# A four-layer graph network on one core: positions counted earlier, index lists by DMA, own scores placed in the node stage, and a larger descriptor room

## What is computed

```python
def L0(feat, r_feat, src, dst, W1, b1, W2s, b2s, W2d, b2d, attn):   # 2 heads of 32
    en = (feat @ W2s + b2s).reshape(n, H, F)[src]
    ev = (feat @ W2d + b2d).reshape(n, H, F)[dst]
    e = jnp.sum(leaky_relu(en + ev, 0.2) * attn, axis=-1, keepdims=True)
    m = segment_max(e, dst)
    ee = jnp.exp(e - m[dst])
    alpha = ee / jnp.maximum(segment_sum(ee, dst)[dst], 1e-09)
    msg = softmax(en * r_feat * alpha, axis=-1)
    return (feat + jnp.sum(segment_sum(msg, dst), axis=1)) @ W1 + b1
def L1(x, edge_index):
    return segment_sum(x[src], dst)
def L2(h, edge_index, edge_sh, edge_radial, ...):
    # three small products give 256 weights an edge; tensor-product messages of h[src]
    return h_self + segment_sum(messages, dst) / 4
def L3(h, edge_index, w, fc_w, fc_b, bias):                          # 4 heads
    e = leaky_relu(a_src[:, src] + a_dst[:, dst] + fc_b, 0.2)
    att = softmax of e over the edges of one src
    return mean over heads of segment_sum(att * hp[:, dst, :], src) + bias
```

## Time and profile before

| | us |
|---|---|
| median of 3 runs | 11253.84 |
| the three runs | 11251.82, 11254.23, 11253.84 |
| the profiled execution, its own time | 11248.29 |
| its span in the profile | 11246.5 |
| busy: POOL, DVE | 8106.8, 6482.3 |
| busy: PE, ACT | 3535.6, 3252.6 |

### The profile page before, as it was taken

How to read it: one execution, slowest core, us unless ns; L and a number is a source line. 1 busy time by engine, 2 the same in 40 slices (tenths; PEclk the granted TensorE clock), 3 DMA queues, 4 the chain that set the end, 5 groups by cost and what they waited for, 6 DMA issues and landing times. The chain is left out here.

```text
span 11246.5 us, 94626 instructions
## 1 busy us (share of the span) xinstructions
PE 3535.6 (31%) x22146; PEld 2356.7 (21%) x22342; DVE 6482.3 (58%) x10678; ACT 3252.6 (29%) x5001; POOL 8106.8 (72%) x8498
## 2 busy tenths in 40 slices
PE   3201100056667664000000008888888200000002
PEld 2201100046666563000000003333333100000002
DVE  8738865588888885200000018999999234444442
ACT  0012221145555553011111102222222024334331
POOL 5777777647777777777777767777777577777775
PEclk6555555578888887555555558888888555555555
DMA  7124433311221111111111111111111122222222
GB/s 261 52 86 134 132 107 104 97 53 57 66 66 64 58 66 36 31 26 26 26 26 26 26 35 27 29 29 29 29 29 27 24 53 67 69 72 71 72 72 60
DMA packets 462695, 680.58 MB, mean 61 GB/s; under 512 B 263781, under 2 KB 359878, under 8 KB 424630
## 3 DMA queue, kind: packets, MB, share of 16 engines
q0 software_dynamic: 270016, 149.13, 8.4%
q10 hardware_dynamic: 67072, 346.84, 8.1%
q1 hardware_dynamic: 125558, 184.07, 4.9%
HBM read 368.75 MB, written 310.60 MB: 60 GB/s over the span
## 5 line engine op out<-in xcount | busy, mean ns | idle before, releaser
L1420 POOL DMA_INDIRECT hs<-tab_h,idx x3136 | 2978.6, 950 | 1034.0 <-issue 996.8
L1166 POOL DMA_INDIRECT by_src<-ends,pos_i x1568 | 1564.7, 998 | 643.3 <-issue 487.6
L1985 POOL DMA_INDIRECT hs<-tab_h,idx x1568 | 1480.3, 944 | 518.7 <-issue 518.7
L962 POOL DMA_INDIRECT en<-tab_s,idx x1568 | 1489.2, 950 | 500.2 <-issue 462.8
L683 DVE TENSOR_TENSOR fresh<-fresh,so_far 128x32 f32<-128x32 f32 x294 | 57.6, 196 | 1722.2 <-ACT fresh L1504 1717.6
L1641 PE MATMUL tp_ps<-w_pair,x 128*128 128x512 f32 x1568 | 911.9, 665 | 6.2 <-DVE prod_b L1781 6.1
L1015 PE MATMUL cnt_ps<-hot_hi,hot_lo 128*128 128x98 bf16 x3136 | 287.2, 281 | 1853.3 <-DVE hot_hi L1040 1853.3
L1871 PE MATMUL turn<-ident,both 128*33 128x128 f32 x8 | 1.9, 421 | 2163.3 <-DVEq L1901 2163.3
L1187 PE MATMUL rank_ps<-place_sb,hot_t 128*128 128x98 f32 x3136 | 663.9, 323 | 3.1 <-DVE picked L1321 3.1
L1015 PEld LDWEIGHTS cnt_ps<-hot_hi,hot_lo 128*128 128x128 bf16 x3136 | 250.7, 140 | 1889.9 <-issue 1632.0
L552 PE MATMUL turn<-ident,tails 128*32 128x128 f32 x3 | 1.2, 397 | 2038.5 <-DMA tails<-sums 2038.5
(11 more groups left out here) (347 smaller groups left out, 13731.4 us busy)
## 6 DMA issues: line engine op xcount, KB each, us to landing
sums<-rows ACTq DMA_DIRECT2D x49, 2176.0 KB
sums<-rows ACTq DMA_DIRECT2D x147, 512.0 KB
hs<-tab_h,idx POOLq DMA_INDIRECT x4704, 2.4
ev_rows<-zeros ACTq DMA_DIRECT2D x16, 3136.0 KB
en_rows<-en SPq DMA_DIRECT2D x49, 1024.0 KB, 4.2
en_back<-en_rows ACTq DMA_DIRECT2D x49, 1024.0 KB
raw<-ev_rows ACTq DMA_DIRECT2D x49, 1024.0 KB, 5.0
en<-en_rows SPq DMA_DIRECT2D x49, 1024.0 KB
```

Source lines behind the costliest of these rows:

```text
L962: pool.indirect_dma_start(en[s][:, g, :], None, tab_s0, bass.IndirectOffsetOnAxis(ap=idx[s][:, g:g + 1], axis=0)).then_inc(gathered[s], 16)
L1166: pool.indirect_dma_start(by_src, bass.IndirectOffsetOnAxis(ap=pos_i[k][:, g:g + 1], axis=0), ends[k][:, g, :], None).then_inc(sent[k], 16)
L1420: pool.indirect_dma_start(rows[k][:, g, :], None, tab_h, bass.IndirectOffsetOnAxis(ap=idx[k][:, g:g + 1], axis=0)).then_inc(gathered[k], 16)
L1985: pool.indirect_dma_start(rows[k][:, g, :], None, tab_h3, bass.IndirectOffsetOnAxis(ap=idx[k][:, g:g + 1], axis=0)).then_inc(gathered[k], 16)
```

## The change

1. **Room for descriptors.** The program is built with `dynamic_dma_scratch_size=32768`; it was 16384, the default.

```diff
+    nc = _bacc.Bacc("TRN2", target_bir_lowering=False, num_devices=1, dynamic_dma_scratch_size=32768)
```

```diff
+                    if not known_ge(p, PAIRS - 2):
+                        index(p + 2, s)
+
+
+                def index(p, s):
+                    sp.dma_start(idx[s][:, :], src_i[:, cols2(p)]).then_inc(indexed[s], 16)
+                sp.wait_ge(edges_in, 32)
+                for s in range(2):
+                    index(s, s)
+                turns(sp, body, ahead=2)
...
             @block.gpsimd
             def _(pool):
                 def body(p, s):
 
-                    K.wait(pool, "pool", stored, 16 * (p - 1))
-                    nc.gpsimd.tensor_copy(idx[s][:, :], src_i[:, cols2(p)]).then_inc(indexed, 1)
-                    K.wait(pool, "pool", indexed, p + 1)
+                    K.wait(pool, "pool", stored, 16 * (p - 1), indexed[s], 8 * p + (16 - 8 * s))
                     for g in range(2 * CH):
                         pool.indirect_dma_start(en[s][:, g, :], None, tab_s0,
```

```diff
+        AHEAD, SENT = 16, 6
+        pos_ahead = sb(e0, "pos_ahead", [EP, AHEAD * CH], I32)
+        ends_ahead = sb(e0, "ends_ahead", [EP, AHEAD * CH, 2], I32)
+        sent_ahead = K.own("sent_ahead")
+
+        def send_ahead(pool, t):
+            for n in range(t * CH, (t + 1) * CH):
+                pool.indirect_dma_start(by_src, bass.IndirectOffsetOnAxis(ap=pos_ahead[:, n:n + 1], axis=0),
+                                        ends_ahead[:, n, :], None).then_inc(sent_ahead, 16)
         fd_stack = ExitStack()
...
+                pool.wait_ge(posed_ahead, AHEAD)
+                for t in range(SENT):
+                    send_ahead(pool, t)
...
+                def count(q, lo, hi):
+                    def body(i):
+                        for k in range(2):
+                            t = 2 * i + k
+                            K.wait(dve, "dve", counted, t - 1 + q * (2 * PAIRS + 1))
+                            R.compare(lo, hi, t, k, hots)
+                    pairs(dve, body)
+                count(0, lo_d, hi_d)
+                prefix(0, first_dst, last_dst, has_dst, None)
+                count(1, lo_s, hi_s)
+                prefix(1, first_src, last_src, has_src, base_src)
+                R.start()
+
+                def keep(r, k):
+                    c.link(nc.vector.tensor_copy(ends_ahead[:, cols(r), 0], src_i[:, cols(r)]))
+                    c.link(nc.vector.tensor_copy(ends_ahead[:, cols(r), 1], dst_i[:, cols(r)]))
+                    K.wait(dve, "dve", R.selected, (r + 1) * CH)
+                    c.step(nc.vector.tensor_copy(pos_ahead[:, cols(r)], R.pos[k][:, :]))
+                    dve.sem_inc(posed_ahead, 1)
+
+                def rank_ahead(i):
                     for k in range(2):
-                        t = 2 * i + k
-                        K.wait(dve, "dve", counted, t - 1)
-                        hot(lo_d, hi_d, t, k)
-                pairs(dve, count_dst)
-                prefix(0, first_dst, last_dst, has_dst, None)
+                        r = 2 * i + k
+                        if not first_chunk(r):
+                            R.pick(dve, r * GROUPS - 1, 1 - k, GROUPS - 1)
+                            keep(r - 1, 1 - k)
+                        if not known_ge(r, AHEAD - 1):
+                            R.hot(dve, r + 1, 1 - k)
+                        for q in range(GROUPS - 1):
+                            R.pick(dve, r * GROUPS + q, k, q)
+                    c.restart()
+                R.hot(dve, 0, 0)
+                pairs(dve, rank_ahead, end=AHEAD // 2, ahead=True)
+                R.pick(dve, AHEAD * GROUPS - 1, 1, GROUPS - 1)
+                keep(AHEAD - 1, 1)
+
```

```diff
+            last_rank, RANK_PAIRS, FIRST = last_chunk - AHEAD, PAIRS - AHEAD // 2, AHEAD // 2
...
+                for t in range(SENT, AHEAD):
+                    send_ahead(pool, t)
+
...
+                def message(i, ranks):
                     for k in range(2):
                         t = 2 * i + k
+                        r = t - AHEAD
...
+                        if ranks and not first_chunk(r):
+                            R.pick(dve, r * GROUPS - 1, 1 - k, GROUPS - 1)
+                            send(r - 1, 1 - k, i - FIRST - 1 + k)
...
+                pairs(dve, lambda i: message(i, False), end=FIRST)
+                R.hot(dve, 0, 0)
+                pairs(dve, lambda i: message(i, True), first=FIRST, ahead=True)
+                R.pick(dve, last_rank * GROUPS + GROUPS - 1, 1, GROUPS - 1)
+                send(last_rank, 1, RANK_PAIRS - 1)
```

```diff
+                        for g, at in enumerate(sets):
+                            for b in range(at.start, at.stop):
                                 pool.indirect_dma_start(target[:, b, :], None, table,
                                                         bass.IndirectOffsetOnAxis(ap=rows[:, b:b + 1], axis=0)).then_inc(sums_in[g], 16)
+                        if place:
+                            for g, at in enumerate(sets):
+                                pool.wait_ge(done, g + 1)
+                                for b in range(at.start, at.stop):
+                                    place(pool, b)
                         for g in range(SETS):
-                            pool.wait_ge(sums_in[g], 16 * SET * len(sum_rounds))
+                            pool.wait_ge(sums_in[g], 16 * sizes[g] * len(sum_rounds))
...
+                       place=lambda pool, b: pool.indirect_dma_start(own_rows, bass.IndirectOffsetOnAxis(ap=first_src[:, b:b + 1], axis=0),
+                                                                     a_src[:, b, :], None).then_inc(own_placed, 16))
```

More of the change, by code:

```diff
@@ L107, in pairs @@
 def pairs(eng, body, first=0, end=PAIRS, ahead=False):
-    if first == 0:
-        body(0)
-        first = 1
-    with eng.Fori(first, end - ahead) as i:
+    body(first)
+    with eng.Fori(first + 1, end - ahead) as i:
         body(i)
@@ L116, in pairs, with turns @@
         body(i)
-def turns(eng, body, first=0, end=PAIRS):
+def turns(eng, body, first=0, end=PAIRS, ahead=0):
     if first == 0:
@@ L124, in turns @@
         first = 2
-    with eng.Fori(0, (end - first) // 2) as j:
+    rounds = (end - first - ahead) // 2
+    with eng.Fori(0, rounds) as j:
         body(2 * j + first, 0)
         body(2 * j + first + 1, 1)
-    if (end - first) % 2:
-        body(end - 1, 0)
+    for p in range(first + 2 * rounds, end):
+        body(p, p % 2)
 def known_ge(t, n):
@@ L372, in node_stage @@
                 sum_rounds.append(1)
+            sizes = ENDING if gather else EVEN
+            SET = max(sizes)
+            sets = [slice(sum(sizes[:g]), sum(sizes[:g + 1])) for g in range(SETS)]
             with ExitStack() as st:
@@ L376, in node_stage, with pieces_of @@
                     products.append((h, then[0], then[1]))
-                pieces = [(b, 1) for b in range(SET)] if wide else [(b, min(4, SET - b)) for b in range(0, SET, 4)]
+                def pieces_of(at):
+                    size = at.stop - at.start
+                    return [(b, 1) for b in range(size)] if wide else [(b, min(4, size - b)) for b in range(0, size, 4)]
+                most = len(pieces_of(slice(0, SET)))
                 spread_w, turned_ps, turned, prod = [], [], [], []
@@ new lines, in vector @@
+                for n, row in enumerate(flag_rows):
+                    c.link(nc.vector.tensor_copy(flags_t[:, n, :], row[0:n_heads, :]))
+                c.join()
+                dve.wait_ge(self.exped, 1)
+                totals(1, same, ALU.mult, ALU.add)
+                c.step(nc.vector.tensor_scalar(tot[:, :, :], tot[:, :, :], self.floor, None, ALU.max))
+                c.step(nc.vector.reciprocal(run[:, :, :], tot[:, :, :]))
+                c.step(nc.vector.tensor_tensor(e[:, :, :], e[:, :, :], run[:, :, :], ALU.mult))
@@ L937, in build @@
[L937 to L938 removed]
+            stored, back_in = K.sem("stored"), K.sem("back_in")
+            indexed = [K.sem(f"indexed{s}") for s in range(2)]
+            cleared, added, tilted, scored, hots, counted, copied, summed, starts, chain_v, loaded, posed_ahead = (
+                K.sem(n) for n in ("cleared", "added", "tilted", "scored", "hots", "counted", "copied", "summed", "starts", "chain_v", "loaded",
+                                   "posed_ahead"))
@@ L984, in _ @@
                         act.wait_ge(cleared, 16 * zeroed_pieces)
+                act.wait_ge(starts, 2)
+                R.begin_act(act)
+                def rank_ahead(i):
+                    for k in range(2):
+                        for q in range(GROUPS):
+                            R.count_on(act, 2 * i + k, k, q, AHEAD - 1)
+                pairs(act, rank_ahead, end=AHEAD // 2, ahead=True)
+                act.wait_ge(R.place_out, AHEAD * GROUPS + 1)
+                nc.scalar.copy(base_src[:, :], R.place_sb[0][:, :])
+                act.wait_ge(R.selected, AHEAD * CH)
                 act.wait_ge(placed, ev.PLACED)
```

(29 more changed lines are left out.)

566 lines of the change are left out of this document (293 added, 273 removed).

## The result

The changed kernel takes **10989.42 us** (median of 4 runs, 10983.5 to 10991.1) against 11253.44 (4 runs). The ratio is 0.9765, 95% interval 0.9748 to 0.9782. The forecast was 10,990. A number so near is partly luck. Two terms were off in opposite directions, one by 10 us and one by 8, and the term of the pauses came out right although its reason did not.

The account below looks back on a forecast made before the run. POOL's issuing of 8438 gathers and scatters was taken as the bound. Against a span of 11246.5, -150 - 9 - 23 - 82 = -264 gives 10,982; with run corrections 10,990 us, range 10,940 to 11,100.

Parts of the forecast that it names:

- Pauses: POOL's waits at a full descriptor room: doubling it removes all, -94 us (-12 stage 2, -41 layers 1 and 2, -41 layer 3).
- half of the pauses: Rival, POOL's issue loops: with the doubled room pauses come half as often, +47 us, 11,037; chance 0.20.
- Index lists: Stage 1: SP's DMA replaces 49 copies by POOL, saving POOL their busy time and waits, -33 us.
- Start: Start to first gathers: later first gather against slow gathers and weights' block saved; sum 0, bounds -5 and +5 us.
- Stage 1 on DVE: Counting, 16 ranked chunks, scoring from 1196 at 9.0 us a chunk to 2078; gathers stay the bound, 103 us spare.
- Behind the last gather: After stage 1's last gather (Te): DVE until Te+110; POOL's 96 scatters take 122 us plus 30 from softmax, until Te+152.
- The block's end: End of stage 1's block: 3.0 us and a little for draining, from Te+152 to stage 2's start at Te+156.
- Stage 2: First ranked scatter at Te+382, POOL standing 18 us; then 82 chunks at 20.84 us, last scatter at Te+2091; gain 117.
- Uneven sets: Node stages behind the last gathers: smaller last set shortens waits by 2.5 and 6.5, -9 us, bounds +6 and -20.
- Own placement: Own scores placed in layer 2's node stage fill the 35.6 us wait, 12.5 exposed: -23 us, bounds -15 and -27.
- the dearer softmax: Rival, softmax beside scatters: DVE's chain of 83 grows 60%, scatters stretch to Te+200, some 50 more, 11,040; chance 0.09.
- The slow one: Rival: scoring becomes stage 1's bound, late from 10.05 us a chunk; at 13.5 the kernel takes 11,330; chance 0.03.

Follow-up runs that it names:

- experiment 6: Kernel before the change with a descriptor room of 15360 in place of 16384, nothing else: 11,138.4 us, ratio 0.9902.
- 1: Changed kernel with only the descriptor room put back to 16384: 11,081.7 us when run again; first 15,572 us on the slow chip.
- 7: Changed kernel with the index lists of stage 1 copied by POOL again, SP's index DMAs taken out: 11,048.3 us.
- experiment 9: Changed kernel with own scores placed in layer 3's block again, its node stage keeping the uneven sets: 10,995.7 us.

## Why the prediction was right, step by step

- **Pauses, 94.** Right in size (95 out of the gaps in experiment 6; 92 for the whole in 1), and by luck for 32768. That they cost only where the room fills right behind a group's end bore out at 16384, 17408 and 15360. But the forecast let the doubled room fill after 226 issues, two or three behind a group's end; in fact it is full at 128, exactly 8 groups, where its own argument would have given a pause. It also treated "more room" as the cure and never asked for less; 15360 does as well and a little better. The count from the Trainium skill ("DMA: Bandwidth & Descriptors", section "The descriptor swizzle", given there for a transfer of 1 MiB) agrees with the traces at 15360, 16384 and 17408, and not at 25600 and above, where it gives 177 and more. What a full room costs the page does not say; that half of the pauses would stay was my step from its count. The gain of half that I drew from it did not come: with 32768 there is no pause in any layer, and one of 3.2 us in stage 2.
- **Index lists, -33.** Right in the sum of the first stretch (-33.9), which holds a first gather 5.1 us later than before and slow gathers saved. Taken alone (7) the lists are worth 59, because of pauses that only their combination with the large room brings. This interaction was not foreseen.
- **Start, 0.** The first gather came at 93.3 in place of 88.2, +5.1, the bound of the range; the saved slow gathers gave 5 to 6 back.
- **Stage 1 on DVE.** The scoring took 9.75 a chunk where DVE had not caught up (forecast 9.0), and started at 1136.9 (forecast 1196), because 16 chunks of positions cost 14.0 each and not 19.2: beside messages a chunk costs DVE more than alone. The two errors cancelled. 87 us of margin were left, 103 forecast.
- **Behind the last gather.** DVE's chain: 110 forecast, 110.8 found (2179.8 to 2290.7). The 96 scatters: to Te+152 forecast, Te+151 found. The stretch by the softmax: 30 forecast, 28.7 found, and the reciprocal is free as assumed. Not every operation with one input is: the two issues beside L881 and L882 (0.98 us and less each, `cont_dst` or the like alone) took 1.72 and 1.47. The Trainium skill's sentence that descriptor generation needs only the write side ("SBUF — State Buffer", section "Who interferes with whom") is labelled there as inferred. Issues of 3.0 to 3.5 us beside scans of two SBUF operands speak against it; that such an instruction contends with GpSimd is borne out.
- **The block's end, 4.** Mis-sized: 14.2 us, 10 too low. The term was taken from a block that ended without transfers in flight. Stage 2 started at Te+165, not Te+156.
- **Stage 2.** The path from there to the first ranked scatter took 218 us and not 226. So that scatter came at Te+383, 382 forecast, by two errors against each other (10 and 8 us): that is luck. POOL stood 6.0 and not 18. The rest ran at 20.76 a chunk, 20.84 forecast.
- **Uneven sets, -9.** Found -4.4 in the two stretches counted (-1.9 and -2.5), and, as it seems, another 9 in layer 2's node stage (experiment 9), where the sum had none. The gap rows alone (20.6 to 17.1, 16.6 to 11.9) look like -8, but the 98 fetches took 3.7 and 2.1 longer than before (4287.6 to 4414.3 and 6412.1 to 6538.2, first to last start; before 123.0 and 124.0). All of it is issuing time (busy 94.4 to 98.1 and 95.4 to 97.5): 14 and 11 fetches take over 1.1 us, where 5 and 7 did, and most of the longer time stands beside DVE's L519 and L524 of the normalizing, which now run between the fetches.
- **Own placement, -23.** Found -18.0 in the stretch, of which the placement is 9.7. The term was too large by the part that the sets would have won anyway, and 4 too low in what stays exposed (12.1 + 4.5 against 12.5).

Of the rivals, half of the pauses, all of them and the dearer softmax did not occur. The slow one did not occur on this chip and did on another, where DVE was late already at the counting.

## What to carry to other kernels

When one engine issues thousands of DMAs, subtract the plain gap from its idle time and look at where the rest stands. Pauses with a fixed period, at the same place in a group, hang on how the room for descriptors and the size of the groups meet; try a smaller room as well as a larger one. And when two parts of a change touch the same wait, the sum of their single prices is wrong: give the wait to one of them, and undo each alone to see which.

## What the runs showed of the hardware

- In loops over groups of 16, a room for descriptors of 15360 or 32768 bytes gives no pause, 16384 one in every 112 issues. The largest gaps in the layers' gathers are 0.3, 0.3 and 4.7 us.
- 256 scatters on one semaphore show where a room is full: at 106 transfers with 15360, 113 with 16384, 120 with 17408, and 128 with 25600, 26624 and 32768. The pause there is 3.0 to 5.3 us.
- The end of a block with scatters in flight depends on the room, but not in one way. Stage 1's took 14.2 us with 32768, 11.6 with 16384 and with 15360. Behind stage 2 the changed kernel waited 11.06, 11.06 and 9.75, and the kernel before 13.26 with 16384 and 6.72 with 15360.
- POOL's own copies between gathers bring pauses of 3.1 us with 32768, at the 129th gather and every 96 after, where the same gathers without copies have none.
- One of the chips ran every version a third slower: DVE waited 40 us a turn of its counting loop as long as the gathers of stage 1 ran, and the branch of SP's loop took 700 ns in place of 45 throughout. The median gather of layers 1 and 2 was issued in the same 944 ns there. What slowed the rest was not found.
